# The order of the masked attention's steps: a written-out string of letters replaced by a rule

## What is computed

```
q = (inputs_q @ Wq + bq).reshape(b, s_q, 16, 64) / sqrt(64)
k = (inputs_kv @ Wk + bk).reshape(b, 1601, 16, 64)
v = (inputs_kv @ Wv + bv).reshape(b, 1601, 16, 64)
attn = einsum('bqhd,bkhd->bhqk', q, k)
attn = softmax(where(mask, attn, -1e30))
out = einsum('bhqk,bkhd->bqhd', attn, v).reshape(b, s_q, 1024) @ Wo + bo
x = x + out
```

## Time and profile before

| | |
|---|---|
| median of 3 runs | 4301.44 us (4300.44 to 4301.75) |
| time of the profiled execution | 4301.44 us |
| its span, first to last instruction | 4299.7 us |
| phase `L2a` in the span | about 1216 to 2749 us, eight batches |
| one batch in the middle | 190.70 us |

### The profile page before, as it was taken

One profiled execution on the slowest core, in us unless ns is written; L12 is line 12 of the kernel. 1 busy time (PEld: TensorE's weight loads), 2 busy tenths in 40 slices (PEclk: granted clock), 3 DMA queues, 4 the chain that ended last, 5 costly groups with the idle time before them and its releaser, 6 DMA issues. The chain is left out here.

```text
span 4299.7 us, 72412 instructions
## 1 busy us (share of the span) xinstructions
PE 4007.4 (93%) x26524; PEld 2864.9 (67%) x26524; DVE 2751.3 (64%) x6263; ACT 2777.2 (65%) x4848; POOL 864.2 (20%) x769
## 2 busy tenths in 40 slices
PE   7897899999889999999999999789999999978799
PEld 6654444444467777777777777548888888854467
DVE  7655888888466666566566565465566556548556
ACT  6523667767357667676767677437777777757456
POOL 2100000000000000000000000007777777751100
PEclk9998999999899999999999999899999999989899
DMA  2100433231100000000000000100000000000100
GB/s 72 42 1 26 80 50 51 44 42 15 45 13 1 13 13 1 13 1 13 1 13 13 1 1 1 43 16 9 9 9 9 9 1 1 1 10 1 41 3 8
DMA packets 55898, 78.90 MB, mean 18 GB/s; under 512 B 10164, under 2 KB 47173, under 8 KB 54445
## 3 DMA queue, kind: packets, MB, share of 16 engines
q1 hardware_dynamic: 51084, 67.97, 7.4%
q10 hardware_dynamic: 4464, 6.30, 0.4%
HBM read 51.31 MB, written 4.19 MB: 13 GB/s over the span
## 5 line engine op out<-in xcount | busy, mean ns | idle before, releaser
L2388 POOL TENSOR_TENSOR L3a_p_lo<-L3a_wq,L3a_p_hi 128x512 fp32r<-128x512 f32 (+1 forms) x480 | 625.7, 1315 | 241.0 <-ACT L3a_p_hi L2325 232.2
L1223 DVE CUSTOM_DVE_ANT_0 L2a_sc<-L2a_score,L2a_mask_n 128x804 f32<-128x804 f32 x512 | 500.0, 991 | 211.5 <-issue 194.6
L603 ACT ACTIVATE L1a_work<-L1a_ring 128x1024 f32<-128x1024 f32 x416 | 412.3, 1025 | 164.3 <-PE L1a_ring L435 164.1
L1113 ACT ACTIVATE L2a_pt<-L2a_ring 128x512 f32<-128x512 f32 x768 | 424.5, 597 | 138.4 <-PE L2a_ring L1002 133.3
L717 DVE TENSOR_REDUCE L1a_mx<-L1a_ring 128x2 f32<-128x1024 f32 x384 | 456.5, 1222 | 50.3 <-PE L1a_ring L454 45.6
L1098 ACT ACTIVATE L2a_sc<-L2a_sc,L2a_nb 128x1608 f32<-128x1608 f32 x256 | 418.4, 1636 | 33.9 <-DVE L2a_nb L1228 33.9
L1002 PE MATMUL L2a_ring<-L2a_ident,L2a_sc 128*128 128x128 f32 x3072 | 424.3, 278 | 15.4 <-ACT L2a_sc L1098 9.0
L1002 PEld LDWEIGHTS L2a_ring<-L2a_ident,L2a_sc 128*128 128x128 f32 x3072 | 341.6, 141 | 85.9 <-issue 35.9
L2480 DVE TENSOR_REDUCE L3a_mx<-L3a_ring 128x1 f32<-128x402 f32 (+2 forms) x640 | 316.5, 538 | 120.8 <-PE L3a_ring L2177 113.1
L2324 ACT ACTIVATE L3a_wq<-L3a_ring 128x512 f32<-128x512 f32 (+1 forms) x480 | 284.0, 592 | 148.0 <-PE L3a_ring L2099 104.4
L1017 PE MATMUL L2a_res<-L2a_pt,L2a_v 128*64 128x256 f32 (+1 forms) x3328 | 375.3, 382 | 1.4 <-ACT L2a_pt L1113 1.4
(11 more groups left out here) (743 smaller groups left out, 8713.1 us busy)
## 6 DMA issues: line engine op xcount, KB each, us to landing
L1a_keys<-L1a_k_hi SPq DMA_DIRECT2D x224, 52.0 KB
L1a_kt<-in_ctx_t SPq DMA_DIRECT2D x8, 800.5 KB, 4.4
L2a_ct<-in_ctx_t SPq DMA_DIRECT2D x8, 800.5 KB, 4.3
L1a_keys<-L1a_k_lo SPq DMA_DIRECT2D x112, 52.0 KB
L0a_cx<-in_ctx SPq DMA_DIRECT2D x16, 320.0 KB, 3.9
L3a_cx<-in_ctx SPq DMA_DIRECT2D x16, 320.0 KB, 3.7
L2a_mask_u<-in_mask SPq DMA_DIRECT2D x16, 200.1 KB, 4.5
L1a_scr_q<-L1a_keys SPq DMA_DIRECT2D x3, 1024.0 KB
```

What stands on the lines that cost most here:

```text
L603: act.activation(probs[:, (par * NU + u) % c.PS, :, :], ring[tile][:, :, :], ACT.Exp).then_inc(tile_free[tile], 1)
L1113: ins = act.activation(pt[:, t:t + 4, g // 3, q], bank[:, :].rearrange("p (t q) -> p t q", t=4), ACT.Copy)
L1223: dve.tensor_tensor_reduce(sc[:, two, e, w].rearrange("p (k j) -> p k j", k=2), score[e][:, :, 0:CH], mask_n[:, r % 2, w].rearrange("p (k ...
L2388: pool.tensor_tensor(p_lo[0:r, at % PL, 0:W], probs[0:r, at % 2, 0:W], p_hi[0:r, at % PH, 0:W].bitcast(F32), ALU.subtract).then_inc(part_o ...
```

## The change

`ORDER` and the lists that it draws from go. A rule (`slot`) writes the order instead, one for odd and one for even slots; `beside` hands out the k, q, v, c, x, p and f of a slot, and `upto` spreads them over the slot's places. Both lists hold the same 352 steps with the same batch offsets; no instruction is added or removed, no buffer changes. Slots 8 to 13 of both, written out (a slot begins with its first S and ends ahead of the next slot's; only T keeps its number g, and belongs to slot r - 1, but for T5 in slot 8 before, which belongs to slot 6):

```
--- before.py
+++ after.py
@@ -770,49 +770,87 @@
     RING = ("turn", "turn_x", "query", "key", "value", "spread", "project", "finish")
     SPLIT = ("query", "key")
 
-    KINDS = dict(S="scores", M="max", E="exp", T="turn", V="values", U="sums", R="spread", N="normal", q="query", k="key", v="value",
-                 p="project", f="finish", c="part_c", x="turn_x", n="norm_x", m="mask")
-    ORDER = """
-        STTMqMEvkkSTTMTTMvTEvvEkV
-        SUTMTMTvkRSTMTMNTvEvMT
-        STTMkEvqSMTTTMTTpkkvEU
-        SVEMRTMTkMTTMSTTNEfTfM
-        SMTTqkEvTSTMTTTMkMkEEv
-        SVTMUvMMRNTSTTTTkvETMM
-        STTkqvSEMTTTUTTnEvEMkV
-        SMTTMknvRSMTMTTkT
-        SNETvTMMTkqEvSTTMTTTMkEUvV
-        SEMTTMnkTMRSTTMEvTTN
-        SMTTMkkqETMSTTMTkT
-        SEVMMETTUTkkRMSTTTMqENT
-        STMMTkETMSTUTTTEkkMEV
-        STMMTkTRccSxTNTTTM
-        SEcxMTMMTckqEvSTMTTTTkvEvVEUMk
-        SMMTTmTkvRMSTMTTvNEvmT"""
-
     def __init__(self):
-        rows, pairs, halves = range(self.NR), range(self.NP), range(SH)
-        behind = [(self.NP - 1, -1)] + [(p, 0) for p in range(self.NP - 1)]
-        ahead = [(p, 0) for p in range(1, self.NP)] + [(0, 1)]
-        of = {
-            "scores": [((r, j), 0) for r in rows for j in range(2)],
-            "max": [((r, j, e), 0) for r in rows for j in range(2) for e in range(2)],
-            "exp": [((self.NR - 1, 1), -1)] + [((r, j), 0) for r in rows for j in range(2)][:-1],
-            "turn": [((r % self.NR, g), min(r, 0)) for r in range(-1, self.NR - 1) for g in ((0, 1, 2, 6, 3, 4, 5) if r % 2 else (6, 0, 1, 2, 3, 4, 5))],
-            "values": behind, "sums": behind, "spread": behind, "normal": behind,
-            "query": ahead, "key": [((p, k), off) for p, off in ahead for k in range(4)],
-            "value": [((0, t), 0) for t in range(6, CT)] + [((1, t), 0) for t in range(CT)] + [((0, t), 1) for t in range(6)],
-            "project": [(0, -1)], "finish": [(hf, -1) for hf in halves], "part_c": [(k, 1) for k in range(self.KB)],
-            "turn_x": [(hf, 1) for hf in halves], "norm_x": [(k, 1) for k in range(3)], "mask": [(hf, 1) for hf in halves],
-        }
-        following = {kind: iter(steps) for kind, steps in of.items()}
         self.order = []
-        for letter in "".join(self.ORDER.split()):
-            kind = self.KINDS[letter]
-            n, off = next(following[kind])
-            self.order.append((kind, off, n))
+        for r in range(self.NR):
+            self.slot(r)
         self.ring = Numbered(self.order, self.RING)
         self.split = Numbered(self.order, self.SPLIT)
+
+    def beside(self, r):
+
+        p, odd = divmod(r, 2)
+        ahead = (p + 1) % self.NP, (p + 1) // self.NP
+        before = (p - 1) % self.NP, 0 if p else -1
+        keys = [("key", (ahead[0], 2 * odd + k), ahead[1]) for k in range(2)]
+        first = {14: (0, 3), 15: (3, 6), 0: (6, 10), 1: (10, 13)}
+        second = {2: (0, 1), 3: (1, 2), 4: (2, 4), 5: (4, 6), 6: (6, 8), 7: (8, 10), 8: (10, 12), 9: (12, 13)}
+        values = [("value", (0, t), 1 if r >= 14 else 0) for t in range(*first.get(r, (0, 0)))]
+        values += [("value", (1, t), 0) for t in range(*second.get(r, (0, 0)))]
+        head = [] if odd else [("query", ahead[0], ahead[1])]
+        if r == 13:
+            return keys + [("part_c", k, 1) for k in range(self.KB)] + [("turn_x", hf, 1) for hf in range(SH)]
+        other = {2: [("project", 0, -1)], 3: [("finish", hf, -1) for hf in range(SH)]}.get(r, [])
+        mixed = [t for pair in itertools.zip_longest(keys, values) for t in pair if t]
+        return (head + mixed if r < 14 else mixed[:1] + head + mixed[1:]) + other
+
+    def upto(self, r, k, tasks):
+
+        places = 5 if r % 2 else 10
+        if r in (10, 12):
+            return (0, 0, 0, 0, 1, 2, 2, 2, 2, 2, 3)[k]
+        return k * tasks // places
+
+    def slot(self, r):
+        put = lambda kind, n, off=0: self.order.append((kind, off, n))
+        p, odd = divmod(r, 2)
+        prev, off = (r - 1) % self.NR, 0 if r else -1
+        pair, pair_off = (p - 1) % self.NP, 0 if p else -1
+        tasks = self.beside(r)
+        some = lambda *ks: [put(kind, n, at) for k in ks
+                            for kind, n, at in tasks[self.upto(r, k, len(tasks)):self.upto(r, k + 1, len(tasks))]]
+        turn = lambda *gs: [put("turn", (prev, g), off) for g in gs]
+        if odd:
+            some(0)
+            put("scores", (r, 0))
+            put("max", (r, 0, 0))
+            turn(6)
+            put("max", (r, 0, 1))
+            turn(0)
+            put("spread", pair, pair_off)
+            put("normal", pair, pair_off)
+            turn(1)
+            some(1, 2)
+            put("scores", (r, 1))
+            put("max", (r, 1, 0))
+            put("max", (r, 1, 1))
+            turn(2, 3, 4)
+            some(3)
+            put("exp", (r, 0))
+            turn(5)
+            some(4)
+        else:
+            put("scores", (r, 0))
+            turn(0, 1)
+            some(0)
+            put("max", (r, 0, 0))
+            put("max", (r, 0, 1))
+            some(1, 2, 3, 4)
+            put("exp", (prev, 1), off)
+            some(5)
+            put("scores", (r, 1))
+            put("max", (r, 1, 0))
+            turn(2, 6, 3, 4, 5)
+            put("max", (r, 1, 1))
+            some(6, 7, 8, 9)
+            put("exp", (r, 0))
+            put("values", pair, pair_off)
+            put("exp", (r, 1))
+            put("sums", pair, pair_off)
+        if r in (6, 7, 8):
+            put("norm_x", r - 6, 1)
+        if r >= 14:
+            put("mask", r - 14, 1)
 
 
 class MaskedAhead:
```

## The result

The changed kernel takes 4332.6 us (median of 4 runs, 4328.9 to 4335.3) against 4300.9 us before (4 runs, 4299.6 to 4301.8): ratio 1.0079, 95% interval 1.0066 to 1.0090. It is slower by 0.8%, 31.7 us; the forecast was 4342, with a range of 4316 to 4366.

The account below looks back on a forecast made before the run. TensorE, 187.18 of 190.70 us busy a batch, was taken to set the pace; waits of +0.5 +1.7 +2.4 +0.7 = +5.3 us a batch gave 196.0, +41 us in all, 4342 us, range 4325 to 4366 (4316 with part of a rival).

Parts of the forecast that it names:

- Even slots: Slots 4, 6, 8: 14.74, 14.96, 14.96 us, with waits of 0.2 at T0 for E (slots 6, 8) and 0.19 at T4.
- Odd slots: Slots 5 and 7: 8.80 us each, with the second S at 4.30 us into the slot.
- The claim of T0's bank: Odd slots: k, three places behind T0, waits for T0's bank, 0.32 us in every odd slot.
- Slots 10 and 12: Largest term: M held behind `k_lo`, second S at 4.56 and 5.14 us; slots 10 to 13 take 46.3 against 43.90.
- Rival 1: M of slots 10 and 12 is not late: +1.3 to +2.6 us a batch, 4312 to 4322 us; chance 0.15.
- V behind a single k: Slot 10, second half: no v before V, which waits 0.4 us more for the copy of T5.
- Slots 14 and 15: E and T5's copy of slot 13 stand behind c, c, so T0 waits: 26.5 us against 25.80, +0.7.
- Slots 0 to 3: Same steps, the 3.3 us project ahead of V, 0.32 us wait twice: 52.8 us against 52.26, +0.5.
- rival 2: No change: all waits land under V, 4301 us; chance 0.08.
- rival 3: Faster: four old waits go, -1.7 us a batch, 4288 us, if M of slots 10 and 12 starts by 1.5; chance 0.06.
- Rival 4: The clock falls at longer waits: a tenth of a batch at 1.2 GHz costs 19 us a batch, 4450 us; chance 0.03.
- The rule weighed: TensorE's idle time leaves 3.52 us a batch to win at most; the skill's weight-load share would leave 46 us.

Follow-up runs that it names:

- e5: Slots 0 to 9 of the changed order with slots 10 to 15 of the old order, written out as a list; 4311.2 us, ratio to before 1.0021.
- e3: Changed kernel with R moved in the odd slots: behind k and v in slots 1 to 7, behind k and T1 from slot 9 on; 4324.1 us (one run).
- e6: Changed kernel with both T5 and the last k of slots 9 and 11 put ahead of E; 4343.2 us (one run).
- e1: Changed kernel with the last k of slots 9 and 11 put ahead of E instead of behind it; 4331.8 us, ratio to before 1.0066.
- e2: Changed kernel with the last k of slots 9 and 11 put behind the first two M of slots 10 and 12; 4324.2 us (one run).
- E4: Changed kernel with the last two c of slot 13 moved behind its T5; 4327.3 us (one run).
- e8: A third order of the same 352 steps, arranged by measured step lengths and latencies; 4284.3 us, ratio to before 0.9953.
- e7: Slots 0 to 9 of the changed order with R moved in the odd slots, slots 10 to 15 of the old order; 4300.7 us, ratio to before 0.9998.

## Why the prediction held, and where it did not

- **The method.** Reading the new order slot by slot against measured step lengths gave 196.0 us a batch; 195.22 was measured, against 190.70 before. TensorE's own step lengths did not move: e5 restores the old lengths slot by slot.
- **Even slots.** 14.96 each for slots 6 and 8, measured 14.78 and 14.75, and 14.76 for slot 4 (14.74): the 0.2 at T0 for E was not there in slots 6 and 8. E started about 0.2 earlier than worked out, so that T0 was in time. The wait of 0.19 at T4 is as forecast.
- **Odd slots.** 8.80, measured 8.84 and 8.85. The claim of T0's bank: 0.27 for 0.32, and e3 shows it to be that.
- **Slots 10 and 12.** The wait is the predicted one, and a little shorter (S' at 4.30 and 4.94 for 4.56 and 5.14), with M at 2.24 into slot 10 for 2.49 since E came earlier: M starts as `k_lo` ends. The step that failed is the price of its removal: "If the M were in time, S' would stand at 3.49 in both", 2.7 us less. The prediction left out what holds M next. By its own times T5's copy starts at 8.90 into slot 11 and its bank is free 0.65 later, 1.97 into slot 12, too late for an M at 1.42; by the measured rows 1.7 us is the estimate (under e6). The edits tried won 0.1 (e1) and 0.8 (e2) and lost 0.5 (e6), since each made a new wait. With M in time at 1.41 but E late, the stretch took 46.03, not 43.6. Rival 1, which rested on that price, asked too much of it.
- **V behind a single k.** Forecast 0.4 of wait for the copy of T5, and S' to the next slot 10.34; measured 10.25 in slot 10.
- **Slots 14 and 15.** +0.7, measured +0.8. E4 shows c on ACT ahead of E as the reason for 0.4 of it, all in slot 14, which had grown by 0.5.
- **Slots 0 to 3.** +0.5, measured +0.7.
- **The sum.** +41 us from +5.3 a batch; the phase grew by 35.7 from +4.5, the median by 31.7. The term that was mis-sized is slots 4 to 13: +4.1 forecast, +3.0 measured. The other two were 0.3 too small together and so hid a part of it. The medians grew by 4 us less than the phase of the two profiled executions; no run shows where these 4 us lie, and runs of one kernel scatter by more (last section).
- **What would show it.** "TensorE's idle near 9 us a batch" was wrong as a sign: it is 4.3 us. Most waits turned up as longer busy time. Two slips in the working changed nothing in the sum: the terms of an even slot's second half add up to 10.66, not 10.68, and from `k_hi`'s turn to S' its times give 12.72 - 9.45 = 3.3 us, not 3.6.
- **The other rivals.** No change (rival 2) and faster (rival 3) fell with the M at 2.24 and 2.88 into slots 10 and 12, where rival 3 needed 1.5. Rival 4 fell with the granted clock, 1.00 through the batch in spite of the longer waits.
- **The rule weighed.** By the idle time of the earlier trace rows 3.5 us a batch could be won; the best order tried gained 3.4 (e8), with TensorE idle for 0.9. By the Trainium skill (Perfetto Trace Analysis, Identifying the Most-Contended Engine) the share of the weight loads, beside the share of the peak FLOP/s, is the measure of the distance to the roof. Their busy time is as good as unchanged in e8, 144.26 of 187.32 us, so the 46 us a batch that it leaves open were open to none of the orders here.

## What to carry to other kernels

Where one list orders several in-order engines, work out each engine's start times over one period of the list, from the lengths in the trace, before judging a reordering: it gave this change to 1 us in 195. Before pricing the removal of what holds an instruction, ask what would hold it next, and what the move makes late elsewhere; here the second S of slot 10 stood at 4.30, 4.62, 4.45 and 4.46 with four different orders ahead of it, and the best of them won 0.8 of 4.5 us. A long stretch of one engine's work (V) is where the other engines' backlog is free, so place it right behind the step that creates the backlog, and look at what covers that backlog in the first round, when there is no earlier round to take the V from.

## Hardware behaviour that was not expected

The runs of one kernel scatter by up to 13 us (e5: 4305.6 to 4319.0), while slots that an experiment left alone repeat to less than 0.1 us from one kernel's profile to the next (e5's slots 10 to 15). The self attention phase near the end, the same instructions in every kernel, took 231.3 us in the profile before, 233.8 after (2.5 of the 3.1 us left over above), 226.9 in e7 and 237.3 in e8, and the granted clock over it goes the other way: 0.89 in e7, 0.84 in e8 (second row of the fence above). In e7:

```profile
core 0: us, PE busy (x) PEld busy (x) DVE busy (x) ACT busy (x) POOL busy (x), PEclk, DMA share, GB/s
3834.00:4060.90 226.90, 185.19 (x1408) 109.23 (x1408) 169.01 (x327) 137.28 (x216) 39.13 (x43) 0.89 0.00 1
```

It is a phase with many gaps (TensorE is busy for 185.19 of the 226.90 us), in which the clock changes between its two levels (1.2 and 2.4 GHz), and the same work comes out some 10 us longer in e8, where the lower level lasts longer. That this follows from the moment at which the phase begins, which an edit far ahead of it shifts, was not tested. It means that a change of 5 us in one phase is read from that phase in the trace, not from the total, and that part of what e8 won in its phase (20.7 us) did not reach the median (16.6 us against the 4300.9 above, 19.0 against the runs beside it).

In the changed phase the clock stayed at its upper level over the waits of the batches shown (1.00, with waits of up to 1.2 us). In e8's first batch it did not. TensorE idled 5.39 us up to 1229.44, and for the stretch from 1227.5 to 1234.3 the granted clock is that of the lower level:

```profile
core 0: us, PE busy (x) PEld busy (x) DVE busy (x) ACT busy (x) POOL busy (x), PEclk, DMA share, GB/s
1227.50:1234.30 6.80, 4.86 (x16) 3.95 (x18) 1.81 (x3) 3.29 (x7) 0.00 (x0) 0.50 0.01 2
```

So a fall of the clock as in rival 4 does occur in this phase, beside a wait over four times as long as any in the changed kernel's batch. That the wait caused it was not tested.
